# Attention with ten Sinkhorn steps: the Vector engine reads the younger group's rows and adds their parts, and its long pieces run in two portions

## The reference

```python
def _sot(q):
    qn = q / (jnp.linalg.norm(q, axis=-1, keepdims=True) + 1e-08)
    C = 1.0 - jnp.einsum('bhnd,bhmd->bhnm', qn, qn)
    C = jnp.where(eye, DIAG_VAL, C)
    log_K = -C / OT_REG
    log_marg = -jnp.log(jnp.float32(N))
    log_v = jnp.zeros(q.shape[:2] + (N,), dtype=q.dtype)
    for _ in range(SINKHORN_ITERS):
        log_u = log_marg - jax.nn.logsumexp(log_K + log_v[..., None, :], axis=-1)
        log_v = log_marg - jax.nn.logsumexp(log_K + log_u[..., :, None], axis=-2)
    z = jnp.exp(log_u[..., :, None] + log_K + log_v[..., None, :])
    z = z / jnp.max(z, axis=(-2, -1), keepdims=True)
    return jnp.where(eye, 1.0, z)
attn = jax.nn.softmax(_sot(q) * scale, axis=-1)
out = jnp.einsum('bhnm,bhmd->bhnd', attn, v)
```

## Time and profile before

| | |
|---|---|
| median of 3 runs | 5179.44 us (5171.9 to 5180.66) |
| profiled execution, its own time | 5199.39 us |
| its span in the trace | 5197.3 us |
| Tensor engine busy | 4614.0 us (89%) |
| Vector engine busy | 3760.3 us (72%) |
| Scalar engine busy | 3047.2 us (59%) |
| attention | from about 1250 to about 4090 us |
| one phase in its steady part | 55.74 us |
| mean granted clock of the Tensor engine | 0.931 of full speed |

### The profile page before, as it was taken

The page is one execution under the profiler, slowest core; times in us unless marked ns, Lnnn a source line. Parts: engine busy times, 40 slices in busy tenths (PEclk is TensorE's granted clock), DMA queues, the critical chain, the costliest instruction groups (busy, mean ns, idle before and its releaser), DMA issues. The chain is left out here.

```text
span 5197.3 us, 197824 instructions
## 1 busy us (share of the span) xinstructions
PE 4614.0 (89%) x84561; PEld 3658.4 (70%) x84562; DVE 3760.3 (72%) x8549; ACT 3047.2 (59%) x4474; POOL 314.7 (6%) x349
## 2 busy tenths in 40 slices
PE   5999999895999999999999999999999268599990
PEld 4777777642788888888888888888888244277770
DVE  8999999643677777777777777778787644355557
ACT  4777777533566666656656665666564334377771
POOL 0000000000000000000000000000000014433330
PEclk9999999886999999999999999999999677599995
DMA  1100001032000000000000000000000222322224
GB/s 62 40 26 26 26 26 39 24 102 50 14 22 16 16 16 21 17 16 16 21 17 16 16 19 20 16 16 16 22 12 9 87 76 101 111 66 71 66 63 149
DMA packets 164065, 203.82 MB, mean 39 GB/s; under 512 B 66736, under 2 KB 141744, under 8 KB 160752
## 3 DMA queue, kind: packets, MB, share of 16 engines
q1 hardware_dynamic: 149680, 159.86, 10.3%
q0 software_dynamic: 13632, 32.66, 1.8%
HBM read 123.64 MB, written 68.81 MB: 37 GB/s over the span
## 5 line engine op out<-in xcount | busy, mean ns | idle before, releaser
L653 PE MATMUL y_ps<-k_sb,x_sb 128*12 128x256 f16 x58368 | 1706.1, 275 | 13.1 <-DVE x_sb L890 12.8
L653 PEld LDWEIGHTS y_ps<-k_sb,x_sb 128*12 128x12 bf16 x58368 | 1433.4, 88 | 202.3 <-issue 27.1
L772 ACT ACTIVATE y_sb<-y_ps 128x256 f32<-128x256 f32 x912 | 348.4, 382 | 931.5 <-PE y_ps L653 931.5
L781 ACT ACTIVATE k_new<-cos,k_bias 128x512 f32<-128x512 f32 x768 | 521.0, 683 | 167.1 <-PE cos L680 167.1
L663 PEld LDWEIGHTS turned_x<-rows_in,y_sb 128*128 128x128 f32 x3648 | 478.3, 191 | 118.6 <-issue 71.8
L921 DVE CUSTOM_DVE_ANT_0 plan<-plan,u_rows,v_last 128x512 f32<-128x512 f32 x768 | 535.2, 744 | 6.0 <-issue 0.2
L663 PE MATMUL turned_x<-rows_in,y_sb 128*128 128x16 f32 x3648 | 527.2, 258 | 8.5 <-ACT y_sb L772 8.3
L256 PE MATMUL acc<-w_hl,feat_h 128*128 128x384 f16 x2688 | 455.1, 327 | 87.4 <-ACT feat_h L241 87.4
L886 DVE RECIPROCAL x_sb<-turned_x 128x16 f32<-128x16 f32 x864 | 223.1, 258 | 390.4 <-PE turned_x L663 390.3
L795 ACT ACTIVATE plan<-plan,p_bias,p_scale 128x1024 f32<-128x1024 f32 x384 | 464.2, 1238 | 10.6 <-DVE p_scale L932 10.6
L909 DVE TENSOR_TENSOR plan<-k_sb 128x1024 f32<-128x1024 f16 x384 | 459.7, 1218 | 0.0
(11 more groups left out here) (256 smaller groups left out, 7224.8 us busy)
## 6 DMA issues: line engine op xcount, KB each, us to landing
x_in_sb<-expert_rows SPq DMA_DIRECT2D x39, 528.0 KB
xt<-in_x_dram SPq DMA_DIRECT2D x16, 1280.0 KB, 5.9
q_left<-q_parts SPq DMA_DIRECT2D x192, 64.0 KB, 3.1
q_right<-q_parts SPq DMA_DIRECT2D x192, 64.0 KB, 3.0
y<-expert_results SPq DMA_DIRECT2D x32, 384.0 KB, 3.8
v_parts<-v_sb SPq DMA_DIRECT2D x16, 408.0 KB, 2.4
v_in_sb<-v_parts SPq DMA_DIRECT2D x48, 136.0 KB, 3.5
h_tokens<-h_sb SPq DMA_DIRECT2D x16, 384.0 KB, 2.5
```

Of the source, the lines that this page charges most:

```text
L653: last = nc.tensor.matmul(y[a][32 * c:32 * c + XW, :, :], high[:, j, XW * h:XW * (h + 1)], k_sb[s][:, h, :, at:at + P], start=(h == 0 and ...
L772: nc.scalar.activation(y_sb[a][:, :, :], y[a][:, :, :], ACT.Copy).then_inc(rows_read[a], 1)
L781: nc.scalar.activation(k_new[h % 2][:, c, :], cos[:, c % 2, :], ACT.Exp, bias=k_bias[:, 0:1], scale=1.0 / (REG * Q_SCALE ** 2), accum_out= ...
```

## The change

The rows of the young group are read by the Vector engine. One `tensor_reduce` from `y_ps` adds the product of the high part and that of the low part and writes 128 columns to `y_sb[0]`, where the Scalar engine wrote 2 x 128. `turn(0)` is then one matmul. The old group is left as it was.

The reduction stands at the head of each cycle on the Vector engine. Behind it, and ahead of `scale_of` and `next_x(0)`, stands a first portion of the long pieces; the second portion stands where all of them stood. `low_parts` is cut into two halves.

```diff
-                for part in range(2):
-                    last = nc.tensor.matmul(tr_flat[a], y_sb[a][:, part, :], add_parts, start=(part == 0), stop=(part == 1))
+                for part in range(a + 1):
+                    last = nc.tensor.matmul(tr_flat[a], y_sb[a][:, part, :], add_parts, start=(part == 0), stop=(part == a))
...
-                    if young and i > 0:
-                        read_rows(0, G * YOUNG + (i - 1))
...
+            def add_rows(n):
+                after(dve, product[0], n + 1)
+                nc.vector.tensor_reduce(y_sb[0][:, 0, :], y[0].rearrange("p two n -> p n two"), AX_X, ALU.add).then_inc(rows_read[0], 1)
...
+                    if young and i > 0:
+                        add_rows(G * YOUNG + (i - 1))
+                    if c == 1 and fin:
+                        join(G - 2, new, a, 1)
+                    if c == 2 and fin:
+                        times_u(G - 2, new, a, (2, 3))
+                    if c == 3 and build:
+                        low_parts(G, new, a, 1)
+                    if c == 4:
+                        if f == 0 and tail:
+                            normalise(G - 3, mine, GH - 1, t - 1)
+                        if f == 1 and fin:
+                            normalise(G - 2, new, b - 2, t_fin)
+                        if fin:
+                            times_u(G - 2, new, b, (2, 3))
                     if c == 2 and fin:
                         scale_of(G - 2, a)
...
                         if fin:
                             join(G - 2, new, a, 0)
-                            join(G - 2, new, a, 1)
-                            times_u(G - 2, new, a, (0, 1))
                     if c == 1 and fin:
-                        times_u(G - 2, new, a, (2, 3))
-                        join(G - 2, new, b, 0)
+                        times_u(G - 2, new, a, (0, 1))
                     if c == 2:
                         if build:
-                            low_parts(G, new, a)
+                            low_parts(G, new, a, 0)
                         if fin:
-                            join(G - 2, new, b, 1)
-                    if c == 3:
-                        if f == 0 and tail:
-                            normalise(G - 3, mine, GH - 1, t - 1)
-                        if f == 1 and fin:
-                            normalise(G - 2, new, b - 2, t_fin)
-                        if fin:
-                            times_u(G - 2, new, b, (0, 1, 2, 3))
+                            join(G - 2, new, b, 0)
+                    if c == 3 and fin:
+                        join(G - 2, new, b, 1)
+                        times_u(G - 2, new, b, (0, 1))
                     if c == 4 and build:
-                        low_parts(G, new, b)
+                        low_parts(G, new, b, 0)
+                        low_parts(G, new, b, 1)
```

More of the change, by code:

```diff
@@ L534, in attend @@
         plan = two("plan", [P, TB, TOKENS], F32)
-        y_sb = two("y_sb3", [P, 2, P], F32)
+        y_sb = [sb("y_sb30", [P, 1, P], F32), sb("y_sb31", [P, 2, P], F32)]
         pv_sb = sb("pv_sb", [P, P], F32)
@@ L768, in _, with read_rows @@
             act.wait_ge(consts, START + CONSTS)
-            def read_rows(a, n):
-                after(act, product[a], n + 1)
-                nc.scalar.activation(y_sb[a][:, :, :], y[a][:, :, :], ACT.Copy).then_inc(rows_read[a], 1)
+            def read_rows(n):
+                after(act, product[1], n + 1)
+                nc.scalar.activation(y_sb[1][:, :, :], y[1][:, :, :], ACT.Copy).then_inc(rows_read[1], 1)
             def exponents(G, s, h, chunks):
@@ L816, in phase @@
                     if old:
-                        read_rows(1, (G - 1) * OLD + i)
+                        read_rows((G - 1) * OLD + i)
                         if i == CYCLES - 1:
@@ L932, in scale_of, with low_parts @@
                 nc.vector.reciprocal(p_scale[h % 2][:, :], all_max[:, :]).then_inc(scale_ready, 1)
-            def low_parts(G, s, h):
+            def low_parts(G, s, h, half):
                 after(dve, k_high, (G + 1) * GH + h + 1)
-                nc.vector.tensor_tensor(k_sb[s][:, h, 1, :], k_new[h % 2][:, :, :].rearrange("p b n -> p (b n)"), k_sb[s][:, h, 0, :],
-                                        ALU.subtract).then_inc(k_built, 1)
+                cols = slice(half * 2 * TOKENS, (half + 1) * 2 * TOKENS)
+                done = nc.vector.tensor_tensor(k_sb[s][:, h, 1, cols], k_new[h % 2][:, 2 * half:2 * half + 2, :].rearrange("p b n -> p (b n)"),
+                                               k_sb[s][:, h, 0, cols], ALU.subtract)
+                if half == 1:
+                    done.then_inc(k_built, 1)
             def normalise(F, s, h, image):
```

## The result

| | before | changed |
|---|---|---|
| median | 5180.05 us (5171.9 to 5183.46, 4 runs) | 5296.82 us (5288.91 to 5306.4, 4 runs) |
| ratio to before | | 1.0229 (95%: 1.0203 to 1.0254) |
| profiled execution, its own time | 5199.39 us | 5288.91 us |
| a phase, undisturbed | 55.74 us | 57.41 us |
| mean granted clock of the Tensor engine | 0.931 | 0.928 |

What follows compares the result with a forecast made beforehand. The Tensor engine, working without holes, was taken as the bound. Full phases +92, phases 0 and 1 -4, the phase with an old group alone about +2: together +90 us, 5269 us against the median; range 5240 to 5327.

Steps and rivals of the forecast that it cites:

- The bound: Steady phase of 55.74 us: the Tensor engine's own work without holes; what it sheds is won whole, waits lost whole.
- The gain of turn(0): One product less in each of 432 young turns, 0.22 us each: 1.98 us a full phase, 95 us in all.
- The reduction: Vector engine's new `tensor_reduce` of 128x256 to 128x128: 0.43 us, occupying the engine for 0.33 us.
- c = 4: Cycle 4 of a group: `head_max` behind more Vector work, `max_to_rows` 1.59 us later, twice a full phase, 3.18 us.
- T: Start of `multiply(0)` in a cycle, from which the prediction counts its times in us.
- c = 2: Cycle 2: last two chunks and `head_max` behind the reduction, `max_to_rows` 0.40 us late, twice a phase, 0.80 us.
- The sum of a phase: Full phase: +3.18 + 0.80 - 1.98 = +2.00 us; over 46 phases, +92 us.
- Phases 0 and 1: First two phases: they only gain, 18 x 0.22 = -4 us.
- The clock and the turns: Rival, chance 0.12: Tensor clock falls at one in four of 92 new waits, 2.5 us each, +58, 5327 us.
- this change leaves them alone: Tensor engine's waits of some 4 us at the turns of the program loop: claimed untouched by the change.
- Where nothing was late: The reduction ends before `turn(0)` needs it at T + 3.60, tightest slack 0.3 to 0.4 us; x is in time.
- The other side: Rival, chance 0.06: maxima not late, four waits of a phase under 1.98 us; with no new waits 5084 us.

Runs made afterwards that it cites:

- the mended kernel: Changed kernel, three chunks of `times_u` moved to the tails of c = 1 and c = 3, the last with `head_max` right behind the reduction: 5094.3 us, ratio 0.9836.
- the kernel with waits of 0.93 and 1.18 us: Kernel before, with the Vector engine's pieces cut and placed as in the changed kernel, but no reduction and both products in `turn(0)`: 5293.6 us.
- the fill: Mended kernel plus nine matmuls whose results nobody reads, ahead of `max_to_rows` in the last cycle before each turn of the program loop: 5071.7 us, ratio 0.9775.

## Why the prediction was right, and what it missed

**The bound** was read rightly: the Tensor engine without holes, each hole lost whole, each product won whole, as long as no turn of the loop lies in the phase and the clock stays up.

**The gain of turn(0)**, 0.22 us: the changed kernel has 0.24 us from `turn(0)` to the next piece (2564.18 to 2564.42), where both products took 0.42 to 0.46; the product put back cost 2.00 us for nine. The choice by starts and not by record lengths was right.

**The reduction**, 0.43 us: 0.42 by its rows. The straight line between 128 and 768 elements held, with pairs that lie 128 elements apart and 128 results. By the figures of the Trainium skill (VectorE: DVE Perf Modes, section The TRN2 errata) it was estimated at 0.39; the measured value is 0.03 above that. The same page's advice (section Rules for kernel authors) to consider restructuring a reduction on a hot path is not borne out here: in the mended kernel the reduction is there 432 times, and an undisturbed phase is shorter by all that the product gives.

**c = 4**: `head_max` at T + 4.97 instead of T + 5.08. The pieces up to the reduction came where they were laid out (0.23, 1.49, 2.83), but `normalise`, set at 0.45 us, took 0.35 from its start to the next chunk: before, a small memset stood between it and the chunk, and now it stands with the first chunk. `max_to_rows` is 1.48 us late instead of 1.59; in the second c = 4 of a phase 1.41, since `turn_x` had delayed it there already.

**c = 2**: T + 3.98 instead of T + 4.01, 0.37 us late instead of 0.40. Mending it took 0.7 us off a phase.

**The sum of a phase**: +3.63 - 1.96 = +1.67 us instead of +2.00, over 46 phases +77 instead of +92. Phases 0 and 1 gained 8 us between the two profiles, where 4 were laid out; in the kernel before the clock was at 0.50 for 15 us of them, in the changed one for 8.

**The clock and the turns** are the term that was mis-sized. I laid the clock out as a rival with a chance of 0.12 and gave nothing to it in the forecast. The attention of the two profiled executions differs by 127 us: 44 phases in the middle make 44 x 1.67 = 74, nine falls of the clock away from the turns 9 x 1.6 = 15, and 13 turns of the loop that cost 2.1 us more 27; the last 10 lie in the first full phase and in the last two, one of which ran 10 us at 0.50 where it ran none before. So the falls were in the right rival, but one in four waits was too many (nine behind the 62 of c = 4 in these 31 phases), and 2.5 us for a fall too dear (1.6). The larger part, the dearer turns, stood in no case: "this change leaves them alone" is the sentence that failed. A turn's idle time went from 4.0 to 5.4 us and its stretch at 0.50 from 6.8 to 10.5. That the time still lies in the range is luck in part: its upper end was set by falls at the waits, which gave 15 us. The Trainium skill (TensorE: Matmul & The Clock Gate, section Loop structure matters more than you think) has the engine go cold on long waits between bursts; this trace shows falls behind waits of 1.26 us, so here it did happen, while the kernel with waits of 0.93 and 1.18 us had none outside its turns.

**Where nothing was late** held: `turn(0)` waits for the reduction nowhere in the steady part, and `x` is in time. **The other side**, maxima in time, did not come; the mended kernels reach it by another order, and not by pieces that overlap more.

## What to carry to other kernels

Before work is moved to an engine with idle time, lay out its queue from the start of a cycle to each result that another engine waits for. A load of 83% did no harm here, while the order of the pieces alone cost 2.28 us in a phase where the change brings 1.98. Where a result is just in time, as `head_max` was to 0.1 us in the profile before, it goes first, and what nobody waits for stands behind it. And a hole in the Tensor engine's work can cost more than its length: the granted clock shows it, and a few matmuls put into the hole tell the two apart.

## What the runs showed that I had not expected

- Nine useless matmuls of 256 columns (1.15 us by their row) ahead of a turn of the program loop shortened the turn from 9.1 us to 5.6, their own time included, and a kernel with no holes away from the turns by 23 us in the median.
- A turn of the loop costs 6.1 to 6.8 us with two products in `turn(0)` and 8.0 to 9.7 with one. In the mended kernel some 2.3 x 13 = 30 us of what the single product was worth went there, until the fill brought them back. The trace shows where the time lies, in longer idle time and a longer stretch at half speed; the cause stays open.
- Doubling the reduction cost 175 us where the queue explains 72: the four holes of a phase only became longer, but the clock then fell in 29 of 31 phases instead of nine, and the falls cost more than the longer holes.
